# Routed transformer layer on one core: three stages behind barriers rewritten as one pipeline of 200 tile steps

## The reference

```
h = layernorm(x) * (1 + cb) + sb
shared   = (silu(h @ shared_gate.T) * (h @ shared_up.T)) @ shared_down.T          # inner width I = 512
probs    = sigmoid(h @ router_w.T + routing_bias)                                # 8 experts
scores, indices = top_k(probs, 2); scores = scores / sum(scores)
combined = sum over the two chosen experts e of score * ((silu(h @ gate_w[e]) * (h @ up_w[e])) @ down_w[e])
x = x + gb * (shared + combined)
```

## Time and profile before

| | |
|---|---|
| median of 3 runs (lowest to highest) | 1727.96 us (1726.53 to 1730.68) |
| the profiled execution: its time, its span | 1720.55 us, 1719.0 us |
| mean granted TensorE clock | 0.985 of full speed |
| busy over the span: TensorE, weight load, VectorE, ScalarE, GpSimd | 96%, 86%, 63%, 47%, 35% |
| attention, shared stage, experts, last stage (from, to) | 0, 627, 902, 1577, 1719 us |

### The profile page before, as it was taken

How to read it: one execution, slowest core, us unless ns; L and a number is a source line. 1 busy time by engine, 2 the same in 40 slices (tenths; PEclk the granted TensorE clock), 3 DMA queues, 4 the chain that set the end, 5 groups by cost and what they waited for, 6 DMA issues and landing times. The chain is left out here.

```text
span 1719.0 us, 35718 instructions
## 1 busy us (share of the span) xinstructions
PE 1643.1 (96%) x10888; PEld 1481.4 (86%) x10889; DVE 1079.3 (63%) x2651; ACT 811.7 (47%) x1583; POOL 600.1 (35%) x671
## 2 busy tenths in 40 slices
PE   8899999999999979999888999999999999997998
PEld 7799999999999978888867888888888888886787
DVE  6777787777778767877763444444444444443576
ACT  5556665665655645454423333333333333333453
POOL 3543444344332013555532333333333333332310
PEclk9999999999999989999998999999999999998999
DMA  3234334433445334222223132144133241112992
GB/s 117 87 111 154 123 111 136 137 115 112 145 144 197 140 113 155 76 85 76 78 72 118 55 98 83 53 128 123 61 107 110 89 129 55 56 52 68 252 228 74
DMA packets 109825, 190.02 MB, mean 111 GB/s; under 512 B 14372, under 2 KB 74404, under 8 KB 109484
## 3 DMA queue, kind: packets, MB, share of 16 engines
q1 hardware_dynamic: 80972, 125.39, 22.8%
q0 software_dynamic: 27648, 61.38, 12.5%
q10 hardware_dynamic: 1120, 2.10, 0.3%
HBM read 106.73 MB, written 82.10 MB: 110 GB/s over the span
## 5 line engine op out<-in xcount | busy, mean ns | idle before, releaser
L806 PE MATMUL e_bank<-w_all,e_xT_hi 128*128 x1088 | 355.0, 407 | 0.3 <-issue 0.2
L806 PEld LDWEIGHTS e_bank<-w_all,e_xT_hi 128*128 128x128 f32 x1088 | 195.4, 189 | 38.9 <-issue 1.7
L1439 ACT ACTIVATE e_y<-e_bank,score 128x256 f32<-128x256 f32 x136 | 64.7, 476 | 332.2 <-PE e_bank L33 332.2
L1414 POOL DMA_DIRECT2D e_h<-x_rows x136 | 75.1, 552 | 402.9 <-PE e_bank L788 372.0
L806 PE MATMUL e_bank<-w_all,e_xT_lo 128*128 x544 | 215.1, 395 | 0.0
L849 DVE TENSOR_TENSOR e_prod<-e_silu_g,e_bank 128x512 f32<-128x512 f32 x136 | 93.5, 688 | 178.2 <-PE e_bank L806 178.2
L843 DVE TENSOR_TENSOR e_aT_lo<-e_bank,e_aT_hi 128x512 fp32r<-128x512 f32 x136 | 94.1, 692 | 152.8 <-ACT e_aT_hi L830 152.8
L658 DVE TENSOR_REDUCE bmax<-s_pair 128x1 f32<-128x512 f32 (+1 forms) x192 | 166.4, 867 | 12.0 <-PE s_pair L33 8.6
L396 ACT ACTIVATE pT_hi<-t_pair 128x512 fp32r<-128x512 f32 (+1 forms) x192 | 135.8, 747 | 77.8 <-PE t_pair L520 76.2
L677 DVE TENSOR_TENSOR pT_lo<-t_pair,pT_hi 128x512 fp32r<-128x512 f32 (+1 forms) x192 | 160.2, 862 | 16.1 <-ACT pT_hi L396 14.1
L389 ACT ACTIVATE prob<-s_pair,negmax 128x1024 f32<-128x1024 f32 x128 | 141.5, 1113 | 57.6 <-DVE negmax L670 51.7
(11 more groups left out here) (281 smaller groups left out, 4314.4 us busy)
## 6 DMA issues: line engine op xcount, KB each, us to landing
w_all<-w_parts SPq DMA_DIRECT2D x84, 256.0 KB, 2.7
e_h<-x_rows POOLq DMA_DIRECT2D x136, 130.0 KB, 2.4
w_parts<-piece_hi SPq DMA_DIRECT2D x27, 512.0 KB, 2.6
w_parts<-piece_raw SPq DMA_DIRECT2D x27, 512.0 KB, 3.6
XS<-in_x SPq DMA_DIRECT2D x32, 256.0 KB, 3.0
XR<-in_x SPq DMA_DIRECT2D x32, 256.0 KB, 2.7
x<-XR SPq DMA_DIRECT2D x32, 256.0 KB, 4.4
Z<-x SPq DMA_DIRECT2D x4, 2048.0 KB, 11.7
```

What stands on the lines that cost most here:

```text
L806: mm = pe.matmul(out[:, 0:I], l, w, start=(c == 0 and k == 0), stop=(c == HC - 1 and k == 2))
```

## The change

`shared_phase`, `experts_phase` and `last_phase` become one function, `ffn_phase`, in a single block: 40 steps with the shared matrices (numbers 0 to 39, `ALL` = 40), 136 blocks of experts (40 to 175), 24 late tiles (176 to 199, `L0` = 176). All 200 go through the same semaphores and buffers, and each engine's program runs from one kind of step to the next. What a stage's end guaranteed is now waited for by semaphore: SyncE waits for `gy_done`, the plan and two rings of scatters before it overwrites the other half of `w_all` with expert 1's matrices; GpSimd waits for the padding, the plan and all its scatters before it loads the first block.

The choice of experts is cut into `choose_first` (6 instructions), `choose_second` (6), `scores` (6) and `place` (8), done in the four steps after the group's last, ahead of `dve_products` of that step; `ranks` moves one step later. The last two groups (`CLOSE`) keep all but `place` in one step, and `place` follows in the next.

Tiles 32 to 39 are prepared as the late ones are: ScalarE normalises, TensorE transposes, ScalarE scales and shifts from PSUM (`single_high`), VectorE makes the low part (`single_low`); VectorE's `scale` and `shift` for them are gone. The sums of `y_rows` go in 32 chunks of two tiles through 8 slots, in order, and the late tiles' shared output is added to `Z` by itself (`gated`, `shared_out`); three chunks are gated and added in two late steps, from late step 3 on.

```diff
-    def pe_turn_rows(pe, m, par, rows):
-        pe.wait_ge(f.rows_ready, f.ready_at(m))
+    def pe_turn_rows(pe, m, par, rows, ready, value):
+        pe.wait_ge(ready, value)
...
-    def pe_down(pe, m, par, weights):
+    def pe_down(pe, m, par, weights, free=None, value=0):
         pe.wait_ge(f.aT_lo_done, m + 1)
-        if inside(m - 2, count):
-            pe.wait_ge(f.y_out, m - 1)
+        if free is not None:
+            pe.wait_ge(free, value)
...
-def shared_phase(nc, d, x1, router_w, router_bias):
+def ffn_phase(nc, d, router_w, router_bias, out):
...
     ALL = STEPS + d.extra
+    NBLK = d.blocks
+    L0 = ALL + NBLK
+    LATE = NT - ALL
...
+    C = 2
+    CHUNKS = NT // C
+    SLOTS = 8
...
         jump = sb("jump", [P, E], F32)
-        PLAN_GROUP = GROUPS - 2
+        PLAN_GROUP = GROUPS - 3
...
+        CLOSE = GROUPS - 2
...
+            sp.wait_ge(plan, PLAN)
+            sp.wait_ge(f.xT_mm, ALL)
+            sp.wait_ge(gy_done, ALL)
+            for i in range(2):
+                sp.wait_ge(sent[i], ONCE * (GROUPS // RING))
...
+            for e in range(1, E):
+                if e >= 2:
+                    end = sp.value_load(d.ends_i[0:1, e - 2:e - 1], min_val=1, max_val=NBLK)
+                    hold(sp, d, f.y_mm, end + ALL)
...
+            def load(k):
+                sp.dma_start(slots[:, k % SLOTS], y_v[0, :, C * k:C * k + C, :]).then_inc(y_in[k % SLOTS], 16)
+            sp.wait_ge(f.y_mm, L0)
+            for s in y_sent:
+                sp.wait_ge(s, 16 * (NBLK // 2))
+            for k in range(SLOTS):
+                load(k)
+            for k in range(CHUNKS):
+                sp.wait_ge(out_done, k + 1)
+                n = C * k
+                sp.dma_start(out[n // TB, :, n % TB:n % TB + C, :], Z[:, d.home(n):d.home(n) + C, :]
+                             ).then_inc(stored, 16)
+                if k + SLOTS < CHUNKS:
+                    load(k + SLOTS)
+            sp.wait_ge(stored, 16 * CHUNKS)
...
+            pool.wait_ge(padded, 16 * (E + 1))
+            pool.wait_ge(plan, PLAN)
             for i in range(RING):
                 pool.wait_ge(sent[i], ONCE * (GROUPS // RING))
...
+            for k in range(CHUNKS):
+                pool.wait_ge(y_in[k % SLOTS], 16 * (k // SLOTS + 1))
+                pool.dma_start(slots[:, k % SLOTS], y_v[1, :, C * k:C * k + C, :], accum_op=ALU.add
+                               ).then_inc(y_sum[k % SLOTS], 16)
...
+            def step(j, par):
+                if isinstance(j, int) and j >= NBLK - 2:
+                    normalise_single(d.extra + par)
+                if inside(j - 2, NBLK):
+                    output(j - 2, par)
+                f.act_products_high(act, j + (ALL - 1), 1 - par)
+                if inside(j + 1, NBLK):
+                    f.act_rows_high(act, j + (ALL + 1), 1 - par)
+                else:
+                    single_high(d.extra)
+                f.act_silu(act, j + ALL, par)
...
+            def down(m, par, weights):
+                if not isinstance(m, int) or ALL <= m - 2 < L0:
+                    f.pe_down(pe, m, par, weights, y_copied, m - (ALL + 1))
+                elif m >= 2:
+                    f.pe_down(pe, m, par, weights, f.y_out, shared_count(m - 2))
+                else:
+                    f.pe_down(pe, m, par, weights)
...
+                if n < STEPS and n % GS == 1 and 0 < n // GS <= CLOSE:
                     ranks(n // GS - 1)
-            f.pe_down(pe, ALL - 2, 0, weights)
-            f.pe_turn_products(pe, ALL - 1, 1)
-            f.pe_down(pe, ALL - 1, 1, weights)
+                if n % GS == 0 and n // GS > CLOSE and n <= STEPS:
+                    ranks(n // GS - 1)
...
+            pe.wait_ge(plan, PLAN)
...
+            def step(j, par):
+                if par == 0:
+                    who[:] = experts(j // 2 if isinstance(j, int) else half(j, 0))
+                e = who[2 + par]
+                down(j + (ALL - 2), par, weights_of(who[par]) if inside(j - 2, NBLK) else shared_weights)
+                f.pe_turn_products(pe, j + (ALL - 1), 1 - par)
+                if inside(j + 1, NBLK):
+                    turn_block(j + 1, 1 - par)
+                else:
+                    turn(L0)
+                pe.wait_ge(d.w_ready, 16 * PIECES * e + 16)
+                f.pe_gate_up(pe, j + ALL, par, weights_of(e))
+            steps(pe, step)
+            for i in range(LATE):
+                m = L0 + i
+                down(m - 2, i % 2, weights_of(who[2 + i]) if i < 2 else shared_weights)
...
+            def routing(n):
+                g, i = n // GS - 1, n % GS
+                if 0 <= g < CLOSE:
+                    (choose_first, choose_second, scores, place)[i](g)
+                elif CLOSE <= g < GROUPS and i == 0:
+                    choose_first(g)
+                    choose_second(g)
+                    scores(g)
+                elif CLOSE <= g < GROUPS and i == 1:
+                    place(g)
 
...
+            def gate_chunk(k):
+                dve.wait_ge(y_sum[k % SLOTS], 16 * (k // SLOTS + 1))
+                gate = rows[:, C * k // TB, 0:H].unsqueeze(1).to_broadcast([P, C, H])
+                dve.tensor_tensor(slots[:, k % SLOTS], slots[:, k % SLOTS], gate, ALU.mult).then_inc(gated_done, 1)
+            def output_chunk(k):
+                own = Z[:, d.home(C * k):d.home(C * k) + C, :]
+                dve.wait_ge(gy_done, max(ALL, C * k + C))
+                dve.wait_ge(gated_done, k + 1)
+                dve.tensor_tensor(own, own, slots[:, k % SLOTS], ALU.add).then_inc(out_done, 1)
...
             for n in range(ALL):
                 if n == 2:
                     offsets(NB - 1, NB - 1)
-                if n + 2 < ALL:
+                if n + 2 < STEPS:
                     scale(n + 2)
                 if n >= 2:
                     gated(n - 2)
-                if n + 2 < ALL:
+                if n + 2 < STEPS:
                     shift(n + 2)
                 if n >= 2:
                     shared_out(n - 2)
...
-                if n + 1 < ALL:
+                if STEPS <= n + 1 < ALL:
+                    single_low(n + 1 - STEPS)
+                elif n + 1 < STEPS:
                     f.dve_rows_low(dve, n + 1, (n + 1) % 2)
+                else:
+                    rides(0, 0)
+                    f.dve_rows_low(dve, ALL, 0)
+                routing(n)
+                if n == STEPS + 1:
+                    dve.tensor_copy(free_i[:], base[0:1, GROUPS, :]).then_inc(free_known, 1)
                 f.dve_products(dve, n, n % 2)
                 if n < STEPS:
                     add_logits(n)
-                if n % GS == 0 and 0 < n <= STEPS:
-                    place(n // GS - 1)
-                if n % GS == GS - 1 and n < STEPS:
-                    choose(n // GS)
-                if n == STEPS:
-                    dve.tensor_copy(free_i[:], base[0:1, GROUPS, :]).then_inc(free_known, 1)
                 if n == STEPS + 2:
                     plan_ends()
                 if n == STEPS + 3:
...
+            def step(j, par):
+                if not inside(j - 2, NBLK):
+                    gated(j + ALL - 2)
+                f.dve_products_low(dve, j + (ALL - 1), 1 - par)
+                if inside(j + 1, NBLK):
+                    f.dve_rows_low(dve, j + (ALL + 1), 1 - par)
+                else:
+                    single_low(d.extra)
+                if not inside(j - 2, NBLK):
+                    shared_out(j + ALL - 2)
...
+            for i in range(LATE):
+                m = L0 + i
...
+                while chunk < CHUNKS - 1 and 2 * (chunk + 1) <= 3 * (i - 2):
+                    gate_chunk(chunk)
+                    output_chunk(chunk)
+                    chunk += 1
```

724 lines of the change are left out of this document (279 added, 445 removed).

## The result

The changed kernel takes 1679.42 us (median of 4 runs, 1678.08 to 1680.94), the kernel before 1728.12 us beside it: a ratio of 0.9717, 95% interval 0.970 to 0.9734. That is 48.7 us, and 2.6 us above the 1676.8 us of the forecast, inside its range.

A forecast was written before the change was run, and what follows sets the result against it. TensorE was taken as the bound everywhere, its waits and low clock as the losses. 18.3 + 12.7 + 21.4 - 1 - 0.2 = 51.2 us off the 1727.96 us median gives 1676.8 us, range 1668 to 1690 (8 in 10).

The forecast's parts named there:

- What bounds the kernel: All stages: TensorE is the bound everywhere; only its waits and time at the lower clock can be won.
- The step into the experts: Shared stage to fourth block: 32.21 us become four steps, 19.5 us, gain 12.7, first block's load hidden by 3 us.
- The step into the late tiles: Last block to sixth late tile: 50.65 us become six steps, 29.2 us, gain 21.4 us.
- The sums in chunks of two: Late stage: VectorE busy 4.4 of 4.87 us on the mean; cost 0, at most 0.3 in each of ten steps.
- The 1 us for the first chunk: Late stage's start: VectorE asks 10.6 us after transfers start, chunk comes at about 11; 1 us lost, between 0 and 5.
- The turn of the ring: Late stage, rival: eight slots turn too slowly, deciding from 26 us on; at 40 us, 1733 us total; chance 0.03.
- The rule weighed: Late stage: the skill page's 2.6 us per transfer speaks against halving chunks; 48 more transfers counted as none, since slots overlap.
- The routing: Shared stage: choice cut in four fits VectorE's idle 1.93 us; 229.42 us become 211.1, gain 18.3.
- the burst of step 28: Shared stage, group 6 still chosen in one step: TensorE loses 1.3 us waiting, plus 1.2 us of clock.
- Step 32: Shared stage, last group's burst: no router matmuls, 1.1 us shorter, so 2.3 us lost.
- The plan: Shared stage, five steps from 857.67: now costs 5.7 us, 4.4 left after VectorE drops some scale and shift.
- The distance to the median: Whole kernel: runs' median lies 7.4 us above the profiled 1720.55 us; this distance is kept in the forecast.

The follow-up runs named there:

- direct_before: Kernel before with the shared stage's 128 indexed scatters replaced by plain transfers to fixed places: 1726.08 us, ratio 1.0 to the kernel before.
- direct_after: Changed kernel with its 128 indexed scatters of the shared stage replaced by plain transfers to fixed places: 1678.23 us, ratio 0.9726 to the kernel before.
- chunks_of_four: Changed kernel with sums in 16 chunks of four tiles through four slots: 1768.43 us, ratio 0.9781, 0.15 us from the changed kernel on that chip.
- sigmoid_later: Changed kernel with ScalarE's sigmoid of a group moved behind the next step's normalise: 1787.07 us, ratio 0.984 to the kernel before.
- both_again: Changed kernel with the sigmoid behind the next step's normalise and group 6 also spread over four steps: 1776.94 us, ratio 0.9848 to the kernel before.
- spread_only: Kernel before with only the choice of experts spread over four steps for groups 0 to 5, stages kept: 1815.45 us beside 1814.94, ratio 0.9997.

## Why the prediction was right, and where it was not

**What bounds the kernel.** Right. TensorE's waits were the losses, and with them its low clock, which went from 0.96 and 0.94 in the first and last stage to 0.99 and 1.00; taking them away brought 48.7 us.

**The step into the experts, 12.7 us.** Right to 0.1 us. The cover was thinner than said. GpSimd began group 5's scatters at 811.69 (predicted 803.9: the low clock lasted longer and six quarters had overrun), went on with group 6 without a pause and then waited 2.22 us for group 7's places, until 855.25, so they ended at 877.7 and not 865.7. The load followed at 880.93, 3.2 us behind them (predicted 3.4); at 2.4 us the load lands at 883.3, where TensorE asks at 883.83. 0.5 us in hand and not 3. TensorE did not wait there in any trace.

**The step into the late tiles, 21.4 us.** Right: 50.65 - 29.20 = 21.45. Between direct_before and direct_after it is 21.1, and the step into the experts 12.7 again.

**The sums in chunks of two.** Right that transfers do not bound this stage, and chunks_of_four shows that their size is free. The 1 us for the first chunk was a wait of VectorE of 1.0 us (until 1571.44) that cost TensorE nothing: the steps around it are 4.86 to 4.88 us long. The one longer step, 5.20 us from 1634.64, is one with two chunks, as the prediction allowed. The turn of the ring is measured now: 14.0 us with four slots. With eight, load and accumulation take 12.1 us in place of 9.7, which makes some 16.4 (an estimate from these), against the 26 us from which it decides.

**The rule weighed.** The Trainium skill, DMA: Bandwidth & Descriptors, Anatomy of one DMA, has 2.6 us for such a transfer. The traces do not agree: 5.4 and 6.7 us with eight slots, 4.3 and 5.4 with four. Halving the number of transfers (chunks_of_four) moved the time by 0.15 us and no late step by more than 0.33 us, so that nothing was rightly put down for their number.

**The routing, 18.3 us.** The mechanism was right, and two terms were mis-sized. The first is the sentence "all put exactly into this idle stretch. I therefore cost them at nothing": the idle 1.93 us had been read in a step in which `scale` does not wait for a `normalise` that stands behind the sigmoid, and the first quarter falls in the one step of four in which it does. 0.58 x 6 = 3.5 us; sigmoid_later and both_again show it. The prediction had the bound (0.5 us for each of six groups) and took zero. The second is the burst of step 28: 1.3 us of wait and 1.2 of clock predicted, but the wait was 2.64 us and the clock of the window 0.89, and this step and the next took 10.97 + 7.07 us where 6.64 + 5.98 would have been the undisturbed ones, 5.4 us and not 2.5. The 1.3 us more of wait are the same misreading once more: "VectorE's idle time begins ... 2.46 us after a transpose" was 3.78 us in step 28, and 2.39 in sigmoid_later, where `ranks` waits 1.21 us. The other 1.6 us are clock. Step 32, which has no `scale`, came out right in this trace: its choice begins after 2.32 us, `ranks` waits 2.26 us (2.3 predicted), and the step takes 7.91 us against 4.87 + 0.66 + 2.3. The loss of clock moves about, though: in direct_after steps 28, 29 and 32 take 10.56, 5.98 and 9.30 us, the same in all to 0.1 us. The plan came out right too, 28.54 us for its five steps where 28.75 were predicted. 3.5 + 2.9 - 0.2 = 6.2 us.

**The distance to the median.** I had kept the 7.4 us between the profiled execution and the runs as a constant of the kernel. It was not: the changed kernel's profiled execution lies 1.3 us below its own median, and some 4 us of the 7.4 were the luck of the stage's start. The two errors worked against each other: against the profiled executions the forecast has 51.2 - 42.5 = 8.7 us too much gain (6.2 in the routing and 4.2 at the stage's start, less 1.7 that the other stretches give), and in the distance it has 6.1 too much, which leaves the 2.6 us. So that the forecast came within 2.6 us is in part luck. Between direct_before and direct_after, both profiled within 0.5 us of their medians, the seven stretches of the table give 0.2, 0.1, 14.5, 12.7, -1.3, 21.1 and 0.6, together 48.0 us: there the shared stage is 3.8 short of the forecast, and the end gives 1.8 more than the forecast.

**Left open.** The experts take 1.0 us more, in seven steps of 5.0 to 5.37 us that the trace gives no wait for; the kernel before has five such steps, of up to 5.30. What the two further edits are worth where engines are not held up was not measured. By the traces the moved sigmoid gives 3.5 us at the first quarters and up to 4.1 at step 28 (10.97 + 7.07 us against 7.96 + 5.98; an estimate, since in sigmoid_later a long wait falls into the next step), and spreading group 6 as well would then add only the rest of the 5.4. Whether the first block's rows then come late is open too, as no run of them met such a chip; I have no version that is shown to beat the changed kernel.

## What to carry to other kernels

Read the slack of an engine in the very step in which it is to be filled: what is idle in an ordinary step may be spent in the one that has a table load ahead of it. Where stages meet at a barrier, the time from the last regular step to the first regular step, less the regular steps that lie between, was the whole gain to 0.1 us, twice (to 0.3 us in a second pair of traces). A profiled execution can be several us off its own runs, so its distance to the median belongs in the range and not in the sum.

## What the runs showed of the hardware

- On three of the chips, ScalarE, VectorE and TensorE stood still for as much as 17.7, 13.5 and 12.6 us at a time while GpSimd issued a group's indexed scatters, one every 1.26 us, beside straight-line code: 78 to 90 us per launch. With plain transfers of the same tiles, on one of these chips, no such wait was left. The loop of the experts, with 136 such scatters, one every 4.87 us, was spared. The cause behind it is open.
- Where the engines are held up, spreading the choice in the three stages of before gained nothing (spread_only, ratio 0.9997), and the changed kernel gained 36 us (29 to 49) and not 48.7.
- At the start of the shared stage the granted clock rose from 0.50 to 1.00 between 635 and 638 us in three traces and between 645 and 648 in the other eleven, so that the same step took 7.2 or 9.67 us.
- Transfers of 256 KB landed after 5.4 and 6.7 us with eight slots in flight and after 4.3 and 5.4 us with four: less in flight did not pay in proportion.
